# Moving a router's small exponential, its row stores and a loop's code in a tuned transformer block with experts

## The reference, cut to what matters

```python
x = x + _L0_xcond_ref(_layernorm(x), cond[:, None, :], ctx, ...)   # adaln, mha, adaln, mha, adaln, glu_ff
x = x + _L0_ffn_ref(_layernorm(x), wqkv, w1, w2)

# in mha
scores = jnp.einsum('bhqd,bhkd->bhqk', q, k) / math.sqrt(DH)
attn = jax.nn.softmax(scores, axis=-1)
# in _L0_ffn_ref
attn = jax.nn.softmax(q[..., :, None] * k[..., None, :], axis=-1)
logits = jnp.einsum('bsej,bsj->bse', attn, v).reshape(-1, E)
top_logits, idx = jax.lax.top_k(logits, 2)
scores = jax.nn.softmax(top_logits, axis=-1)         # the two gates of a token
he = jax.nn.silu(a) * g @ w2[e].T                    # a, g = split(x_rep @ w1[e].T)
out = out + jnp.where((expert_ids == e)[:, None], he, 0)
```

## Time and profile before

| what | value |
|---|---|
| median of three runs | 1936.63 us |
| profiled execution, span | 1933.32 us, 1931.3 us |
| busy share: PE, ACT, DVE, POOL | 91%, 67%, 68%, 45% |
| one round in the loop | 90.8 us |
| first tile of the experts | at 1548.9 us of the span |
| mean granted clock of TensorE | 0.979 |

### The profile page before, as it was taken

How to read it: one execution, slowest core, us unless ns; L and a number is a source line. 1 busy time by engine, 2 the same in 40 slices (tenths; PEclk the granted TensorE clock), 3 DMA queues, 4 the chain that set the end, 5 groups by cost and what they waited for, 6 DMA issues and landing times. The chain is left out here.

```text
span 1931.3 us, 67493 instructions
## 1 busy us (share of the span) xinstructions
PE 1750.5 (91%) x25740; PEld 1523.0 (79%) x25740; DVE 1310.6 (68%) x3351; ACT 1293.0 (67%) x2517; POOL 860.6 (45%) x1038
## 2 busy tenths in 40 slices
PE   5798889999999999999999999999988889889996
PEld 3677768788888888788778788888776678888995
DVE  4455747687878787777777777878665565465565
ACT  4476666776777776767777777777665656566663
POOL 2232324444444535353544444444434264656554
PEclk9999999999999999999999999999997899999998
DMA  5101111211111111122121211111133121222266
GB/s 171 51 20 45 51 40 34 65 49 49 49 49 49 49 49 58 43 62 64 40 61 42 70 45 55 49 49 49 46 79 103 34 69 46 64 56 74 75 204 206
DMA packets 127894, 123.66 MB, mean 64 GB/s; under 512 B 14153, under 2 KB 102121, under 8 KB 127786
## 3 DMA queue, kind: packets, MB, share of 16 engines
q1 hardware_dynamic: 119018, 105.04, 19.2%
q0 software_dynamic: 8768, 17.20, 2.7%
HBM read 82.56 MB, written 40.67 MB: 64 GB/s over the span
## 5 line engine op out<-in xcount | busy, mean ns | idle before, releaser
L1827 POOL TENSOR_TENSOR pr<-pr,sm 128x512 f32<-128x512 f32 x256 | 269.2, 1071 | 494.7 <-DVE sm L1367 493.8
L1092 ACT ACTIVATE kp<-ps 128x512 f32<-128x512 f32 x512 | 296.5, 610 | 25.5 <-PE ps L271 12.3
L1111 ACT ACTIVATE pr<-pr 128x512 f32<-128x512 f32 x256 | 159.6, 629 | 195.7 <-DVE pr L1360 190.1
L1357 DVE TENSOR_REDUCE mx<-ps 128x8 f32<-128x512 f32 x256 | 172.4, 673 | 152.0 <-PE ps L770 151.9
L783 PE MATMUL ps<-WO,os 128*128 128x128 f32 x2048 | 245.4, 278 | 16.4 <-issue 14.6
L783 PEld LDWEIGHTS ps<-WO,os 128*128 128x128 f32 x2048 | 235.9, 192 | 23.8 <-issue 21.0
L891 PE MATMUL ps<-xT,wt 128*128 128x128 f32 (+1 forms) x1728 | 219.4, 276 | 7.4 <-DVE wt L1646 5.7
L891 PEld LDWEIGHTS ps<-xT,wt 128*128 128x128 f32 (+1 forms) x1728 | 201.5, 183 | 11.0 <-DVE wt L1646 7.3
L1092 ACT ACTIVATE vp<-ps 128x512 f32<-128x512 f32 x256 | 141.8, 596 | 93.5 <-PE ps L271 93.5
L1365 DVE TENSOR_REDUCE sm<-pr 128x8 f32<-128x512 f32 x256 | 169.4, 662 | 24.1 <-ACT pr L1111 23.9
L1360 DVE TENSOR_TENSOR pr<-ps,mx 128x512 f32<-128x512 f32 x256 | 177.1, 692 | 8.8
(11 more groups left out here) (226 smaller groups left out, 3519.7 us busy)
## 6 DMA issues: line engine op xcount, KB each, us to landing
mod<-emb_s SPq DMA_DIRECT2D x96, 256.0 KB, 4.0
xr<-rows_s SPq DMA_DIRECT2D x144, 66.0 KB
cb<-y_s SPq DMA_DIRECT2D x32, 256.0 KB
x_in<-in_x_dram SPq DMA_DIRECT2D x16, 256.0 KB
xn_s<-x_in SPq DMA_DIRECT2D x16, 256.0 KB, 2.0
y1r<-xn_s SPq DMA_DIRECT2D x16, 256.0 KB
y_s<-y1r SPq DMA_DIRECT2D x16, 256.0 KB, 2.0
c_in<-in_ctx_dram SPq DMA_DIRECT2D x16, 256.0 KB, 4.7
```

The lines of the kernel that those rows point to most:

```text
L1092: return nc.scalar.activation(o, i, ACT.Copy)
L1111: nc.scalar.activation(pr[:, p, :], pr[:, p, :], ACT.Exp, scale=SCALE).then_inc(exp_done, 1)
L1357: nc.vector.tensor_reduce(mx[:, p % 2, :], heads(SCORED[p][:]), AX_X, ALU.max).then_inc(max_done, 1)
L1827: tensor(v, v, sm[:, p, :].unsqueeze(2).broadcast_to([P, HG, 64]), ALU.mult).then_inc(prob_done, 1)
```

## The change

Four places are edited. ScalarE takes `gate_exp` of a chunk at the start of the next slot (slot (c + 4, 0), behind the four copies of weighed results) instead of at the end of slot (c + 3, 3); in slots with u = 0 it takes all four exponentials ahead of the first copy of values. VectorE does `gates` in the next slot too, between the second and the third `peak`. GpSimd issues two of the eight row stores ahead of the probabilities and six behind, where it was four and four. For the last chunk ScalarE takes `gate_exp` at position 4 of slot (18, 3), where it was position 8. ScalarE's bodies 8 to 11 are written out, where they were a loop.

```diff
@@ ScalarE, slot(i, u)
                         weighed_out(li, lu, b)
+                if u == 0 and ok(i - 4):
+                    gate_exp(i - 4)
                 if u == 0 and ok(i - 3):
                     out_glu(i - 3)
                 if here:
                     for p in range(NT):
                         exp(i, u, p)
-                        if p > 1:
+                        if p > 1 and u:
                             values_out(i, u, p - 2)
...
-                    for t in range(2, NT):
+                    for t in range(2 if u else 0, NT):
                         values_out(i, u, t)
...
-                             (3, 2, ... glu_act(c, 3)), (5, 2, ... glu_split(c, 3)), (8, 3, gate_exp))}[u]
+                             (3, 2, ... glu_act(c, 3)), (5, 2, ... glu_split(c, 3)), (4, 3, lambda c: c_last(c) and gate_exp(c)))}[u]
@@ ScalarE, the experts
-            with act.Fori(EARLY_TILES // TB, START[1] - 1) as d:
+            for d in range(EARLY_TILES // TB, START[1] - 1):
                 tiles_act(d)
@@ VectorE, slot(i, u)
+                    if u == 0 and p == 2 and ok(i - 4):
+                        gates(i - 4)
                     if here:
                         peak(i, u, p)
...
-                             ..., (7, 0, norm2), (8, 3, gates))}[u]
+                             ..., (7, 0, norm2), (8, 3, lambda c: c_last(c) and gates(c)))}[u]
@@ GpSimd, slot(i, u)
                     rows_ready(i - 4)
                     scatter(0, 0)
-                    scatter(1, 0)
-                hooks = {0: ((4, 4, lambda c: scatter(0, 2)), (6, 4, lambda c: scatter(1, 2)), (8, 3, lambda c: ln_rstd(3, c))),
+                hooks = {0: ((4, 4, lambda c: scatter(1, 0)), (5, 4, lambda c: scatter(0, 2)), (6, 4, lambda c: scatter(1, 2)), (8, 3, lambda c: ln_rstd(3, c))),
```

More of the change, by code:

```diff
@@ L1281, in slot @@
                          3: ((0, 2, lambda c: c_last(c) or glu_act(c, 2)), (1, 2, lambda c: c_last(c) or glu_split(c, 2)),
-                             (3, 2, lambda c: c_last(c) or glu_act(c, 3)), (5, 2, lambda c: c_last(c) or glu_split(c, 3)), (8, 3, gate_exp))}[u]
+                             (3, 2, lambda c: c_last(c) or glu_act(c, 3)), (5, 2, lambda c: c_last(c) or glu_split(c, 3)), (4, 3, lambda c: c_last(c) and gate_exp(c)))}[u]
                 for h in range(HG + 1):
@@ L1705, in slot @@
                          3: ((0, 3, top_second), (1, 2, gated(glu_mul, 2)), (1, 3, counts), (2, 2, gated(glu_split_lo, 2)), (3, 0, stats2), (4, 2, gated(glu_mul, 3)),
-                             (6, 2, gated(glu_split_lo, 3)), (place_at(i - 3)[1], 3, place_out), (7, 0, norm2), (8, 3, gates))}[u]
+                             (6, 2, gated(glu_split_lo, 3)), (place_at(i - 3)[1], 3, place_out), (7, 0, norm2), (8, 3, lambda c: c_last(c) and gates(c)))}[u]
                 if isinstance(i, int) and (i, u) == (NC, 0):
```

## The result

The changed kernel is slower: 1963.9 us median of four runs (1957.4 to 1969.3), against 1934.7 for the kernel before in the same comparison, a ratio of 1.0143 with a 95% interval of 1.0111 to 1.0174. The forecast was 1917 (1903 to 1938), with a chance of 0.07 for this side. The profiled execution took 1969.3 us, its span is 1967.4.

A forecast was written before the change was run, and what follows sets the result against it. TensorE, busy 91% of the span, was taken as the bound, so gains had to be its idle time. 10.6 + 11.6 - 9.6 + 4.9 = 17.5 us off 1933.3, plus about 1 for the median: 1917 us (1903 to 1938).

The forecast's parts named there:

- step 4: Row stores two ahead of the probabilities, six behind: last turned probability's copy falls inside the run, costing 0.8 us a round.
- step 1: Exponential behind the copy os, start of slot (i, 0): scores no longer wait for its table load, 0.88 us a round gained.
- step 3: Fourth exponential ahead of the values in slot (i, 0): layer norm's h earlier, TensorE's wait shrinks, 0.97 us a round gained.
- full hold: Rival: signals held until 0.9 us behind the last store, six stores cost 2.1 us a round, 1931 to 1933; chance 0.30.
- Step 2: VectorE's gates between two peaks: about 0.6 us on the softmax's chain, covered by 1.3 us before TensorE needs keys; costs nothing.
- step 5: ScalarE's written-out bodies 8 to 11: fewer table loads, 4.9 us gained; the exponential goes four tiles earlier at the same price.
- Step 6: Rounds 17 and 18: slot (18, 0)'s store run is split, later tiles get longer runs; nothing, +-4 us.
- The rule of the Trainium skill: VectorE and GpSimd block each other at a shared SBUF port pair; last stores stretched 1.3 us, step 4 costing 2.1.
- all turned probabilities are held: Slower rival, copies pt in slot (i, 0): signals held from the first turned product, last copy 2.4 us later, 1957 us; chance 0.07.

The follow-up runs named there:

- spread_gate8: The changed kernel with the row stores spread three, one, one, one, two and the last chunk's gate_exp back at position 8 of slot (18, 3): 1929.2 us, ratio 0.9959.

## Why the prediction was wrong, step by step

**The step that failed is step 4**, the price of six stores in a row, and with it the gains of steps 1 and 3, which stand ahead of the same hold. For a round the forecast was 0.88 + 0.97 - 0.8 = 1.05 us won, and 1.6 were lost. Of this miss of 2.7 us 1.1 is step 4's price, and 1.6 is gain that didn't come with four and four either (0.3 of 1.85). Both are lost at the last turned probability: against the changed kernel with its stores spread, six in a row cost 43.87 - 40.99 = 2.9 us a round, more than the 2.1 of the full hold. The profiled execution is 53.6 us from the forecast (36.1 lost, 17.5 to be won): 29.0 of them in the loop, 14.1 in the tile phase (9.2 lost, 4.9 to be won), 10.5 in the other rounds.

"Between 0 and 2.1 I take 0.8": the six stores cost 43.79 - 42.26 = 1.5 us a round alone, and 43.87 - 41.99 = 1.9 beside the other parts (a part of it at the lower clock). Two things were off. The price with a full hold was worked out as one late copy; by its own numbers that makes 746.4 - 744.8 = 1.6 us and a copy 0.3 earlier than before, and the 2.1 needs one more copy ahead of the last, which the text doesn't name. The hold caught two of the four turned tiles, it ended 1.35 us behind the last store instead of 0.9, and ScalarE then had two more copies ahead of the last: 23.6 us into the slot instead of the 22.6 of the full hold. And the price of four in a row was taken from 0.28 us of idle time. That row shows how long ScalarE stood still, not what it meant for the chain: the copy at 745.22 was let go 0.8 us behind the last store, and the last copy stands 1.45 us behind it, in the kernel before (20.92 and 22.37 us into the slot) as with the exponentials alone moved (20.88 and 22.33). The last copy at 746.67 was "past the run's end", but tied to one that wasn't.

**Step 1** (0.88 us a round): the mechanism was right ahead of the stores. The scores start 0.13 us ahead of the weighing's end:

```profile
642.83 2.10 PE L750 MATMUL ps<-pt,vp 64*64 64x64 f32 x128
...
644.80 2.14 PE L770 MATMUL ps<-kp 64*64 64x64 f32 x128
```

Alone it gave 0.4 us. I had let the gates' delay fall on GpSimd's stores and asked only whether their landing was late, not what they hold: the last one ended 21.3 us into the slot instead of 20.1.

**Step 2** (nothing): right. The keys weren't late; the first store started at 7.45 us, against some 7.0 worked out.

**Step 3** (0.97): the mechanism was right (h at 13.3 us, the wait at L790 0.29, against 13.5 and 0.45), the gain was 0.2 alone, for the same reason as step 1's. Steps 1 and 3 together gave 42.26 - 41.99 = 0.3 us a round with four and four. With the stores spread besides it was 1.3 (40.99), and step 3 with the spread, without step 1, gave the same 1.3 (41.00). So step 1 isn't shown to bring anything there, and no run spreads the stores alone: how the 1.3 divides between the spread and the order of the exponentials is open.

**Step 5** (4.9 us): bodies 8 to 11 take 75.0 us instead of 78.8, 3.8 less. But with gate_exp and gates alone moved, and the loop left, they took 74.8, and the trace has no table load in that loop: with Silu's table already in when the loop begins, none is placed in its body. So beside the moved exponential the rewriting was redundant; in two kernels where the exponential wasn't moved, it brought 1.4 and 2.8 us. The intervals of 3.55 us between two tiles are gone from these bodies, as forecast, but two of 2.6 to 3.4 us are left in each.

**Step 6** (0 +- 4): far too low. The tile phase lost 9.2 us although bodies 8 to 11 won 3.8, so the other tiles lost 13.0. Bodies 0, 4 and 7 take 4.4, 2.0 and 3.5 us more, the first and the last at a clock of 0.93 where it was 1.00. With gate_exp alone moved, bodies 0 and 7 lost 2.6 and 3.5 too. In body 7 it is the exponential's and Silu's table loads (1.9 us at a like clock) and the lower clock, as spread_gate8 shows; "at the same price" in step 5 left out that the body that now takes the loads becomes longer. What makes bodies 0 and 4 longer isn't separated.

**The rule of the Trainium skill** (SBUF - State Buffer, section "Who interferes with whom") was not what cost. Step 4 worked out from it that the stores beside VectorE's statistics would be stretched; they weren't. The section itself is narrower than step 4 has it: it infers that the issuing of a store needs the write side of the shared pair, which an operation of two tensors doesn't take, and the trace agrees. Of the six, which took 967 ns on average, the two beside the statistics (at 661.95 and 663.22) took 0.96 us each, like those ahead of them.

```profile
L1922 POOL DMA_INDIRECT rows_s<-rows,ridx x6 | 5.8, 967 | 1.7 <-issue 1.7
```

**The rivals.** The slower one, "all turned probabilities are held" (1957 us, chance 0.07), is what happened for half of them. Its time is near the measured 1963.9, but partly by luck: its condition, a hold that begins less than 4.3 us into a run, wasn't met (two copies came on time and the third, whose product ended 4.8 us in, didn't), and 19 of the 36 us lost lie outside the loop. The question it asked, where in a run the hold begins, was the right one. With the earlier trace rows in the profile, where longer runs had waits of 1.22 and 3.64 us, its chance was far too low. The chances were spread over sizes of one cost whose nearest long case, 3.64 us, lay outside all but one of them.

## What to carry to other kernels

When a queue shows that an engine was told late, everything behind that point is already late: read how late the last item of the chain is, not how long the engine stood idle. If a gain ahead of such a point is to be kept, take the hold away first; here the two steps were worth 0.3 us a round with the stores in a row, and 1.3 together with the spread. Indirect stores by GpSimd are better put singly between its other work than in a run, above all beside the last small piece that TensorE needs.

## What the runs showed of the hardware

- Three indirect stores of 128 rows a round (959 ns each) to a tensor that nothing reads made the kernel 2.9% longer (1974.6 us against 1919.7 without them), three plain ones from the same queue (569 ns each) made no difference that can be told (1918.1). What suffers is TensorE: ScalarE hears of its products late (up to 3.6 us of idle time), and its own row of matmuls is broken by pauses (0.26 to 0.94 us in the rounds read here). In the changed kernel no wait of VectorE's beside the six stores stands out.
- A hold mostly ended 0.8 to 1.35 us behind the end of the run's last store; with gate_exp alone moved the last copy came ahead of that end in four of eleven rounds. A single store between two other operations showed none. Where in a run a hold begins isn't the same: in the runs of slot (i, 0) no copy of a turned probability due in the first 1.9 us was late, in a run of two a copy due after 2.0 us came 0.8 late in two of eleven rounds and weighing stood still from 2.6 us on, and in the run of six a copy mostly still came on time at 4.5 us. Whether TensorE's signals are held or its program stands still, the records can't tell; that isn't settled, nor what the stores and TensorE share.
- With an idle stretch of 2.7 us and the broken weighing behind it went, in 4 of 11 rounds, a granted clock below 1.00 (0.86 in one) in the second slot; six others had the same stretch at 1.00, and the loop's first round a shorter one, of 1.3 us. It was the same four rounds in the changed kernel and in the one with SyncE's transfers later, one execution of each. Why these four isn't known.
